# One core, gated cross-attention and a mixture of experts: four issuing orders changed at once

## What is computed

```python
x = x + tanh(g_xattn) * xattn(layernorm(x), ctx_768, ...)   # 16 heads of 8 features
x = x + tanh(g_ffn) * ffn(layernorm(x), w_router, w1, w2)
# xattn: both inputs normalised again, q = xn @ Wq + bq, k and v from the context,
#        w = softmax(q k^T / sqrt(8)) over the 77 rows, y = w @ v
# ffn:   logits = x @ w_router (8 experts), the best two, their softmax as gates,
#        h = square(relu(x @ w1[e])), y = sum over experts of gate[e] * (h @ w2[e])
```

## Time and profile before

| what | value |
|---|---|
| median of 3 runs | 505.31 us (503.33 to 508.22) |
| the profiled execution | 504.38 us, of which its span in the profile is 502.3 us |
| PE busy | 349.9 us, 70% of the span |
| DVE, ACT, POOL busy | 235.0, 171.7, 72.7 us |
| mean granted TensorE clock | 0.768 of full speed |
| transfers | 36.54 MB, mean 73 GB/s |

### The profile page before, as it was taken

The page is one execution under the profiler, slowest core; times in us unless marked ns, Lnnn a source line. Parts: engine busy times, 40 slices in busy tenths (PEclk is TensorE's granted clock), DMA queues, the critical chain, the costliest instruction groups (busy, mean ns, idle before and its releaser), DMA issues.

```text
span 502.3 us, 8704 instructions
## 1 busy us (share of the span) xinstructions
PE 349.9 (70%) x2728; PEld 266.3 (53%) x2728; DVE 235.0 (47%) x899; ACT 171.7 (34%) x394; POOL 72.7 (14%) x136
## 2 busy tenths in 40 slices
PE   0403688986990889547982779827994689989757
PEld 0201465664760757445761657625773567757545
DVE  5505427345641656226551466326551365554513
ACT  1200242443440526223550335313351345445212
POOL 9701003003000130003000030001200011011100
PEclk9955555555896859958797769959598589969979
DMA  1354080045118021450207121171205222123050
GB/s 44 81 94 65 24 127 12 7 89 106 65 34 163 24 67 66 85 133 26 107 24 146 52 65 65 55 147 38 96 20 97 84 65 74 58 62 132 21 170 21
DMA packets 29310, 36.54 MB, mean 73 GB/s; under 512 B 5849, under 2 KB 22874, under 8 KB 29274
## 3 DMA queue, kind: packets, MB, share of 16 engines
q1 hardware_dynamic: 28474, 35.05, 28.0%
q0 software_dynamic: 512, 1.06, 0.8%
q10 hardware_dynamic: 288, 0.00, 0.0%
HBM read 23.14 MB, written 2.23 MB: 50 GB/s over the span
## 4 chain that ended last, share of the span: by engine, by line
PE 47%; SPq 15%; DMA 14%; DVE 12%; issue 7%; POOL 3%; ACT 1%; POOLq 0%; DVEq 0%
SPq L305 11%; PE y L535 10%; DMA gb<-gates_scratch 10%; PE c L488 7%; PE ab L447 5%; PE s L469 4%; PE h L526 4%; SPq L319 3%; PE h L527 3%; PE h L528 3%; PE ab L497 2%; PE ab L429 2%; PE ab L503 1%; DMA x_sb<-in_x_dram 1%; PE ab L510 1%
## 5 line engine op out<-in xcount | busy, mean ns | idle before, releaser
L821 DVE TENSOR_REDUCE negm<-ab 128x4 f32<-128x308 f32 x128 | 60.1, 478 | 92.7 <-PE ab L447 90.6
L688 ACT ACTIVATE p<-s 77x512 f32<-77x512 f32 x128 | 75.2, 588 | 30.3 <-PE s L469 29.8
L936 DVE SCALAR_TENSOR_TENSOR u<-h,gb 128x512 f32<-128x512 f32 x64 | 43.4, 684 | 83.9 <-DMA gb<-gates_scratch 67.3
L535 PE MATMUL y<-w2s,hs 128*128 128x128 f32 x512 | 77.2, 301 | 6.7 <-ACT hs L695 6.7
L469 PEld LDWEIGHTS s<-qs,ks 104*77 104x77 f32 x512 | 71.1, 193 | 15.5 <-issue 8.0
L526 PE MATMUL h<-x_hi,w_lo 128*128 128x512 f32 x64 | 38.3, 598 | 57.0 <-DVE u L936 56.8
L447 PE MATMUL ab<-ks,qs 96*128 96x312 f32 x128 | 62.0, 489 | 21.3 <-DMA qs<-q_lo 15.1
L695 ACT ACTIVATE hs<-u 128x512 f32<-128x512 f32 x64 | 40.1, 628 | 106.4 <-DVE u L936 97.6
L535 PEld LDWEIGHTS y<-w2s,hs 128*128 128x128 f32 x512 | 71.4, 216 | 8.0 <-ACT hs L695 7.5
L469 PE MATMUL s<-qs,ks 104*77 104x128 f32 x512 | 72.9, 278 | 1.9 <-DMA qs<-mT 1.9
L488 PE MATMUL c<-p,vs 77*32 77x128 f32 x1024 | 59.2, 330 | 0.1
(11 more groups left out here) (95 smaller groups left out, 419.4 us busy)
## 6 DMA issues: line engine op xcount, KB each, us to landing
gb<-gates_scratch SPq DMA_DIRECT2D x16, 768.0 KB, 6.0
qs<-q_hi SPq DMA_DIRECT2D x16, 256.0 KB, 5.1
gb<-gates_scratch SPq DMA_DIRECT2D x8, 512.0 KB, 3.6
ks<-k_hi SPq DMA_DIRECT2D x64, 39.0 KB
x_sb<-in_x_dram SPq DMA_DIRECT2D x8, 256.0 KB, 7.4
qs<-q_lo SPq DMA_DIRECT2D x8, 256.0 KB, 6.8
x_res<-in_x_dram SPq DMA_DIRECT2D x8, 256.0 KB, 2.7
out_dram<-y_out SPq DMA_DIRECT2D x8, 256.0 KB, 2.3
```

What stands on the lines that cost most here:

```text
L535: mm = nc.tensor.matmul(bank_y[:, D * b:D * b + D], hs[:, e % 2, T * b:T * b + T], w2s[:, e, :], start=(e == 0 and b == 0), stop=(e == E - ...
L688: nc.scalar.activation(p32[:, c, :], src, ACT.Exp).then_inc(p_done, 1)
L821: nc.vector.tensor_reduce(negm[:, :, c], bank_ab[bank][:, 0:J * NP].rearrange("t (i n) -> t i n", n=NP)[:, :, 0:N], AX.X, ALU.max, negate= ...
L936: nc.vector.scalar_tensor_tensor(out=u[:, e % 2, :], in0=bank_h[e % 2][:, :], scalar=0.0, in1=gb[:, par, e, :], op0=ALU.max, op1=ALU.mult) ...
```

## The change

Four things are changed together.

1. On SP, the part of the gates for experts 5 to 7 is issued in slot 2, right behind the part for experts 2 to 4, ahead of the stacks of slot 3 (in slot 3, behind them, before).
2. POOL issues the loads, the residual rows, the stores and the four transfers of the low keys (`stack_low_k`). Tile 1 is loaded at the very start, by SP. A load is now issued at the end of slot 3, one slot earlier in program order, and DVE takes the statistics in slot 0 rather than in slot 1.
3. The turned attention result goes to columns 256 to 511 of the bank `c`, whose columns 0 to 255 hold the result before it is turned. It no longer has a place in the list of the `ab` banks. The first product with the values of the next batch waits until DVE has read it ("scaled").
4. The loop is written out, so all twelve steps are straight code with waits on constants.

DVE's order within a slot changes too: the routing result is read ahead of the fourth row maximum, and the row maxima are split into high and low part earlier. Two memsets of the output buffer on POOL are dropped, and POOL's memsets of the second half of `ks` now stand behind the low keys of tile 0.

```diff
-    (-1, "turn2"), (0, "s1c2"), (-1, "route2"), (0, "s1d2"), (-1, "o3"), (0, "mT2"), (0, "s1a3"), (0, "s1b3"),
-    (-1, "turn3"), (0, "s1c3"), (-1, "route3"), (0, "s1d3"), (0, "o0"), (1, "v"), (0, "mT3"), (-1, "gates"),
+    (-1, "turn2"), (0, "s1c2"), (-1, "route2"), (0, "s1d2"), (0, "mT2"), (0, "s1a3"), (0, "s1b3"),
+    (-1, "turn3"), (0, "s1c3"), (-1, "route3"), (0, "s1d3"), (1, "v"), (0, "mT3"), (-1, "gates"),
     (1, "s1a0"), (1, "s1b0"),
-    (0, "turn0"), (1, "s1c0"), (0, "route0"), (1, "s1d0"), (0, "o1"), (1, "mT0"), (2, "ctxT"), (1, "s1a1"),
+    (0, "turn0"), (1, "s1c0"), (0, "route0"), (1, "s1d0"), (1, "mT0"), (2, "ctxT"), (1, "s1a1"),
     (1, "s1b1"), (2, "xT"),
-    (0, "turn1"), (1, "s1c1"), (0, "route1"), (1, "s1d1"), (0, "o2"), (2, "k"), (1, "mT1"), (2, "q"),
+    (0, "turn1"), (1, "s1c1"), (0, "route1"), (1, "s1d1"), (2, "k"), (1, "mT1"), (2, "q"),
     (1, "s1a2"), (1, "s1b2"),
 ]
 AB_SHIFT = {name: -shift for shift, name in AB_USES}
-AB_HALF = len(AB_USES) // 2
...
-POST = ["recip", "x1", "stats", "moments", "normed"]
+POST = ["recip", "scaled", "x1", "stats", "moments", "normed"]
...
     Q_DMAS = 3
-    K_DMAS = 3 * J
...
-            step(-1, 1)
-            step(0, 0)
-            step(1, 1)
-            with eng.Fori(1, S // 2 - 1) as pair:
-                step(2 * pair, 0, loop=True)
-                step(2 * pair + 1, 1, loop=True)
-            for i in range(S - 2, S + 2):
+            k = sum(len(ab_order(t, S)) for t in range(-2, step)) + ab_order(step, S).index(name)
+            return k % 2, k // 2 + 1
+
+        def steps(step):
+            for i in range(-2, S + 2):
                 step(i, i % 2)
 
         def ffn_units(i, j):
...
-            def load(s, par, loop=False):
-
-                if loop or s >= 2:
-                    sp.wait_ge(norm_d, at(NORM, s - 2, "x_normed"))
+            def load(s, par):
+                sp.dma_start(ctx_sb[:, par], ctx_v[s]).then_inc(first_in[par], 16)
+                sp.dma_start(x_sb[:, par], x_v[s]).then_inc(first_in[par], 16)
+
...
+                for term in (0, 2):
                     for i in range(J):
...
-            def store(s, par):
-                sp.wait_ge(y_added, s + 1)
-                apart(sp)
-                sp.dma_start(out_v[s], y_out[:, par]).then_inc(stored[par], 16)
...
+            load(1, 1)
...
+                    if j == 1 and exists(i - 1):
+                        spread_gates(i - 1, 1 - par)
+                        broadcast_gates(i - 1, 1 - par, 0)
+                    if j == 2 and exists(i - 1):
+                        broadcast_gates(i - 1, 1 - par, 1)
+                        broadcast_gates(i - 1, 1 - par, 2)
                     if j == 3 and third:
-                        stack_k(i + 2, par, 0, loop)
-                        stack_k(i + 2, par, 1, loop)
-                        stack_q(i + 2, par, 0, loop)
-                        stack_q(i + 2, par, 1, loop)
-                        if not loop and i < 0:
+                        stack_k(i + 2, par)
+                        stack_q(i + 2, par, 0)
+                        stack_q(i + 2, par, 1)
+                        if i < 0:
                             unit_rows(par)
-                    if j == 1 and exists(i - 2, loop):
-                        store(i - 2, par)
-                    if j == 1 and exists(i - 1, loop):
-                        spread_gates(i - 1, 1 - par)
-                    if j >= 1 and exists(i - 1, loop):
-                        broadcast_gates(i - 1, 1 - par, j - 1)
-
-            steps(sp, step)
+
+            steps(step)
             for par in range(2):
-                sp.wait_ge(stored[par], 16 * (S // 2 + 1))
+                sp.wait_ge(stored[par], 16 * (S // 2))
 
...
+                        pe.wait_ge(post_d, at(POST, n - 1, "scaled"))
...
+            def turn_heads(s, par, j):
+                n = G * s + j
+                pe.wait_ge(o_taken, n + 1)
+                if n > 0:
+                    pe.wait_ge(post_d, at(POST, n - 1, "scaled"))
+                for r in range(2, 4):
+                    mm = nc.tensor.transpose(bank_c[:, T * r:T * r + T], oT[:, T * r - 2 * T:T * r - T], ident[:, :])
+                mm.then_inc(o_turned, 1)
...
+            def stats(s, par):
+                if s >= 2:
+                    dve.wait_ge(ctx_in[par], landed(s - 2, par))
+                else:
+                    dve.wait_ge(first_in[par], 32)
...
-                dve.wait_ge(ab_ready[bank], k)
+                view = bank_c[:, 2 * T:4 * T].rearrange("t (h v) -> t h v", v=VC)
+                dve.wait_ge(o_turned, n + 1)
                 nc.vector.reciprocal(rden[:, :].rearrange("t (h o) -> t h o", o=1),
...
-                                        ALU.mult).then_inc(ab_taken[bank], 1)
+                                        ALU.mult).then_inc(post_d, 1)
...
-                    if j == 1 and third and (loop or i > -2):
+                    if j == 0 and third and i > -2:
...
+                    if j == 1 and exists(i - 2):
+                        finish(sf, pf)
                     if near[-2]:
                         routed(*near[-2])
                     take(top_scores)
                     take(post)
+                    take(top_scores)
                     take(post)
+                    take(top_scores)
                     if near[-2]:
                         low_x(*near[-2])
                     take(gating)
                     take(gating)
...
+            def load(s, par):
+                pool.wait_ge(norm_d, at(NORM, s - 2, "x_normed"))
+                apart(pool)
+                pool.dma_start(ctx_sb[:, par], ctx_v[s]).then_inc(ctx_in[par], 16)
+                pool.dma_start(x_sb[:, par], x_v[s]).then_inc(x_in[par], 16)
+
+            def load_rows(s, par):
+                if s >= 2:
+                    pool.wait_ge(post_d, at(POST, G * (s - 2) + G - 1, "x1"))
+                    apart(pool)
+                pool.dma_start(x_res[:, par], x_v[s]).then_inc(res_in[par], 16)
+
+            def stack_low_k(s, par):
+                if s >= 2:
+                    pool.wait_ge(s2_ready, NC * G * (s - 1))
+                    apart(pool)
+                if s < 2:
+                    pool.wait_ge(zeroed[par], 2)
+                bank, n = ab(s, "k")
+                pool.wait_ge(ab_taken[bank], n)
+                apart(pool)
+                for i in range(J):
+                    r = QROWS + HD * i
+                    pool.dma_start(ks[r:r + HD, par, :, i, :].bitcast(F32),
+                                   k_lo[QROWS * i:QROWS * i + QROWS].rearrange("p b n -> p (b n)").bitcast(F32))\
+                        .then_inc(k_lo_stacked[par], 16)
+
+            def store(s, par):
+                pool.wait_ge(y_added, s + 1)
+                apart(pool)
+                pool.dma_start(out_v[s], y_out[:, par]).then_inc(stored[par], 16)
...
-            for par in range(2):
-                nc.gpsimd.memset(y_out[:, par, :, :], 0.0).then_inc(stored[par], 16)
...
+                    if j == 0 and nxt:
+                        load_rows(*nxt)
                     if near[-1]:
                         rstd(*near[-1])
...
+                    if j == 1 and exists(i - 2):
+                        store(i - 2, par)
+                    if j == 3 and third:
+                        stack_low_k(*third)
+                    if j == 3 and i > -2 and exists(i + 3):
+                        load(i + 3, 1 - par)
+
+            steps(step)
```

346 lines of the change are left out of this document (156 added, 190 removed).

## The result

The changed kernel takes 412.8 us (median of 4 runs, 408.92 to 415.11) where the kernel before takes 505.51 us (503.33 to 508.22) beside it: 0.8138 of its time, 95% interval 0.8048 to 0.8228. A second set of runs on another chip gave 412.48 us and 0.817 (0.8119 to 0.8221). The forecast was 406 us, range 386 to 438.

What follows compares the result with a forecast made beforehand. PE was taken as the bound in 46 us of a step, a queue order in the last 11. Gains 57 + 9 + 16 + 10 + 12 less 6 for POOL's issuing make 98; 504.4 - 98 = 406 us, range 386 to 438.

Steps and rivals of the forecast that it cites:

- The stall and the clock behind it: Head of steps 2 to 6: PE's 11.4 us wait for late gates goes, 57 us; slot behind it regains clock, 9 us.
- The statistics: Slot 1 of steps 1 to 5: without DVE's statistics of the coming tile it is 3.2 us shorter, 16 us gained.
- The loads: Loads issued by POOL behind the low keys land nothing to 2.8 us late for six tiles: 5 us lost.
- The turned result: PE's 0.47 us wait for DVE's routing copy, in 28 places, falls away with the bank move: 10 us gained.
- The start: Before the steps: memsets moved 4, output memsets dropped 1.0, queries sooner 2.8, first maxima 3.58, row maxima 0.6: 12 us gained.
- The last store and the tail: End of the kernel: the last store goes over POOL, 0.94 us to issue, 1 us lost.
- The loop: Writing the loop out: nothing taken, up to 3 us either way.
- A step of 39 to 42 us: Sign in the changed profile: a full step from turn to turn, some 58 us before, should last 39 to 42 us.
- starved POOL: Rival, 4%: DVE's work stretches POOL's issuing of transfers, loads come 17.4 us late for six tiles, 510 us.
- The small gains are eaten: Rival, 27%: PE waits at the next bank use instead; only stall, start and half the statistics stay, 427 us.
- The clock holds: Rival, 15%: with fewer pauses PE keeps 2.4 GHz in slot 1, 3 us in each of 6 steps, 388 us.
- No effect: Case, 2%: the whole change leaves the kernel's time within 1%.

## Why the prediction was right

The total came out 7 us above the forecast and well inside 386 to 438. The large term was right for its reason, shown from both sides. The smaller ones were off in both directions, some by more than the total, and that they nearly cancel is luck.

- **The stall and the clock behind it, 57 + 9.** Right: 67.3 us in the old kernel, 51.5 when the late gates are put back into the new one. The second is less than the first. A step that stalls gives the loads time to land, which takes three waits of 5.8 us away, and behind its stall slot 1 lasts 7.8 to 7.9 us at a clock of 1.00 in steps 2 to 5, where the changed kernel has 7.8 to 10.2.
- **The statistics, 16.** The step that failed is the cover: "what hides the statistics in slot 0 is DVE's idleness there". DVE is idle, but their data aren't there. With the loads as they are the move is worth nothing (410.31 against 412.8 and 412.48), with early ones 8 to 13 us, and then the cover is complete. PE's wait for the gates' turn fell from 2.50 us to 1.4, 0, 0.3 and 1.4 in steps 2 to 5, and so under 1 in two of the four. The 3.2 us a step were also read off two slots at different clocks.
- **The loads, 5, range 0 to 17.** Mis-sized: 13 to 17. The delay itself was about right (in the step shown DVE waited 0.6 us for the context and 1.6 for the rows, 2.4 and 2.2 at most). What I left out is that DVE's wait passes on to PE through the row maxima queued behind it, that the clock fell behind two of the three such waits in steps 2 to 5 (10.00 us for 8.42 in the slot shown), and that the third tile's load stands on the path at the start, 3.7 + 4.2 us. I had priced the landing rightly at the slow end, 7.4 us, and taken the quick end for the sum "because the long queue of gates is no longer in front". The transfers landed in 7.4 us all the same.
- **The turned result, 10.** The wait has gone, 13 us of it, but not by the step named: with the result back in the shared banks it is 0.3 us. The experiment that undid the bank gave 7 us, of which some 4 are PE's own work and not a wait. So the number is near the 10 taken, and the reason for it was wrong; DVE's order, which the sum did not price, is the likelier one and was not run alone.
- **The start, 12.** 9.7: the first turn is at 68.98 where it was at 78.64. The queries' last piece is issued at 25.50 instead of 33.30, 7.8 us sooner, which is what the first three terms come to (4 + 1.0 + 2.8). Mis-sized is the fourth, DVE's 3.58 and the 0.6 of the row maxima: the rest is 1.9 us, since the load of the third tile is late here too. With early loads the first turn is at 65.33, 13.3 us sooner than before.
- **The last store and the tail, 1.** Mis-sized: from the last turn to the end the old kernel takes 30.4 us and the new one 35.7. Two pieces stand in the timeline of the tail. The gates' way through memory takes 3.88 us from the issue of the write to that of the read-back, where it took 1.40; in the second execution of the changed kernel it takes 2.07, and its tail is 34.0 us, so this part varies between executions. First before, then after:

```profile
476.95 0.32 SPq L331 DMA_DIRECT2D gates_scratch<-gatesT  x1
478.35 1.27 SPq L338 DMA_DIRECT2D gb<-gates_scratch  x3
...
498.77 0.69 DVE L942 TENSOR_TENSOR y_out<-x,y 128x512 f32<-128x512 f32 x1 [2.14 <-PE y L535]
499.55 0.39 SPq L344 DMA_DIRECT2D out_dram<-y_out  x1
```

```profile
375.53 0.83 POOL L1072 DMA_DIRECT2D out_dram<-y_out  x1
376.50 0.32 SPq L300 DMA_DIRECT2D gates_scratch<-gatesT  x1
380.38 1.28 SPq L307 DMA_DIRECT2D gb<-gates_scratch  x3
...
401.07 0.69 DVE L911 TENSOR_TENSOR y_out<-x,y 128x512 f32<-128x512 f32 x1 [2.14 <-PE y L498]
403.30 0.75 POOL L1072 DMA_DIRECT2D out_dram<-y_out  x1 [26.93 <-issue]
```

  A store of 256 KB is issued 1.0 us ahead of that write. And the last store is issued 1.54 us after DVE's last result, where SP issued it 0.09 us after (DVE ended at 499.46); from DVE's end to the end of the span 2.9 us became 5.4, in both executions of the changed kernel. I had counted what POOL takes to issue, not what it takes to begin.
- **The loop, 0.** Right: 1.0019.
- **A step of 39 to 42 us.** Measured 40.4 on the mean, 38.2 to 43.0; in the second execution 42.6.

Of the rivals, *starved POOL* (510 us) is refuted where it was to be seen: 0.58 us for a low key transfer and 0.80 for a large one, beside a DVE busy 56% of the time. The warning of the Trainium skill, "SBUF — State Buffer", section "SBUF: two separate sides", did not come true for these transfers. The same section's exclusive lock does fit the pair 4.87 and 1.12 us of the start, where POOL's own memset ran and took 2.2 us, as it did alone; which mode these instructions of DVE ran in is not in the trace.

*The small gains are eaten* (427) was half right: the statistics' gain was eaten, wholly, by one named wait, and the total lies nearer to my sum because the rest came. *The clock holds* (388) is refuted as a whole: of the slots 1 of steps 2 to 5 two ran at 0.94 and 1.00 and two at 0.56 and 0.66, and every slot 2 at 0.68 to 0.82. *No effect* is refuted.

From the profiled 436.5 us (old kernel, gates early) to 407.1 it is 29.4: 9.5 at the start (first turn at 78.45 and 68.98), 22.7 in 31 slots, less 2.8 in the tail (32.9 and 35.7 us). Of the 22.7 the waits of PE explain 17.1, and the 0.13 us a slot of the turned result some 4, an estimate. The clock from the first turn to the last was 0.86 in the one and 0.83 in the other, so it may have taken something back; that was not taken apart.

## What to carry to other kernels

Take the stretch in which every compute engine stands still, find the transfer that ends it, and look what was issued ahead of it on the same queue: moving one transfer ahead of twelve of keys and three of queries was worth 67 of 93 us. When work is moved earlier, ask first whether its data are there at the new time, and add the engine that waits behind it; a load should be issued by its landing time (7.4 us here) and not by that of its issue (0.8). And an order between two transfers that nothing enforces, like the queries and the weights at the start, can turn over through a delay of 4 us elsewhere and cost more than the delay.
